# A one-core flamingo layer (cross attention and 64 experts): batch 13 routed within the last attention tiles, and loads and first steps reordered

## The reference

```python
x = x + tanh(g_xattn) * xattn(layernorm(x), ctx)      # ctx: 16 x 375 x 128
x = x + tanh(g_ffn) * ffn(layernorm(x))
# xattn: q = rope((x Wq) w_kc_q), scores with rope(ctx) over R = 64 dims, softmax, 16 heads, w_kc_kv, Wo
# ffn: router logits (64 experts), top 8, softmax of the 8; silu(gate) * up, down, weighted sum;
#      and a shared expert times sigmoid of a gate
```

## Time and profile before

| what | us |
|---|---|
| three runs | 1521.08, 1515.08, 1515.82 |
| median | 1515.82 |
| the profiled execution, its time | 1517.49 |
| its span, first to last instruction | 1515.7 |
| TensorE busy in it | 1414.5 (93%) |
| mean granted TensorE clock | 0.977 |

### The profile page before, as it was taken

One profiled execution on the slowest core, in us unless ns is written; L12 is line 12 of the kernel. 1 busy time (PEld: TensorE's weight loads), 2 busy tenths in 40 slices (PEclk: granted clock), 3 DMA queues, 4 the chain that ended last, 5 costly groups with the idle time before them and its releaser, 6 DMA issues.

```text
span 1515.7 us, 25085 instructions
## 1 busy us (share of the span) xinstructions
PE 1414.5 (93%) x7682; PEld 1159.0 (76%) x7682; DVE 1147.5 (76%) x2602; ACT 672.3 (44%) x1558; POOL 781.9 (52%) x857
## 2 busy tenths in 40 slices
PE   6999899999999999999999999986499999989987
PEld 5767788877788787778887768865389998989743
DVE  5777785298988279988539988545488999989588
ACT  3332684011377011177301137331377787767521
POOL 4555674055676458877347886326144343334322
PEclk9999999999999999999999999997699999999999
DMA  8899896456698767740267762396899999999598
GB/s 250 295 317 321 263 286 190 136 177 190 209 293 254 245 200 246 251 125 8 95 226 230 240 225 88 96 351 211 247 341 312 349 355 359 372 342 344 204 426 365
DMA packets 164648, 380.10 MB, mean 251 GB/s; under 512 B 20233, under 2 KB 55715, under 8 KB 162723
## 3 DMA queue, kind: packets, MB, share of 16 engines
q1 hardware_dynamic: 136470, 286.33, 56.9%
q0 software_dynamic: 20608, 62.28, 12.0%
q10 hardware_dynamic: 7436, 29.88, 5.9%
HBM read 238.82 MB, written 139.59 MB: 250 GB/s over the span
## 4 chain that ended last, share of the span: by engine, by line
PE 72%; DMA 10%; DVE 9%; issue 4%; POOL 3%; ACT 2%; SPq 1%; POOLq 0%; ACTq 0%; DVEq 0%
PE bank L828 18%; PE bank L830 17%; PE bank L829 17%; PE bank L932 9%; DMA p_in<-parts 4%; PE bank L961 4%; PE bank L1130 2%; DMA w_ex<-in_w_ex 2%; DMA parts<-y_sb,to_row 2%; POOL slot_rows L1991 1%; PE bank L920 1%; PE bank L1046 1%; PE bank L910 1%; DVE prob_t0l L1320 1%; ACT prob L1734 1%
## 5 line engine op out<-in xcount | busy, mean ns | idle before, releaser
L1969 POOL TENSOR_TENSOR q_rope<-q_rope,q_sin 128x448 f32<-128x448 f32 x192 | 215.4, 1151 | 127.4 <-DVE q_sin L1285 127.1
L2049 POOL DMA_INDIRECT parts<-y_sb,to_row x140 | 137.6, 983 | 222.2 <-ACT y_sb L1875 192.9
L1975 POOL TENSOR_TENSOR prob<-prob,row_inv 128x375 f32<-128x375 f32 x219 | 176.7, 813 | 89.5 <-DVE row_inv L1307 87.1
L1285 DVE TENSOR_TENSOR q_sin<-bank,sin_q 128x448 f32<-128x448 f32 (+1 forms) x256 | 158.0, 617 | 4.0
L1991 POOL DMA_INDIRECT slot_rows<-rows,pos_i x112 | 110.0, 982 | 97.4 <-DVE count L1395 70.0
L932 PE MATMUL bank<-q_rope,m_w 128*128 128x448 f32 x384 | 155.7, 541 | 2.8 <-issue 1.8
L1299 DVE TENSOR_REDUCE row_max<-bank 128x1 f32<-128x375 f32 x224 | 118.5, 534 | 37.7 <-PE bank L830 37.3
L1734 ACT ACTIVATE prob<-bank,row_max 128x375 f32<-128x375 f32 x224 | 128.3, 573 | 9.1 <-DVE row_max L1299 9.1
L1875 ACT ACTIVATE y_sb<-bank,own 96x512 f32<-96x512 f32 (+4 forms) x140 | 91.2, 687 | 68.8 <-PE bank L830 61.1
L961 PE MATMUL bank<-ident,prob 128*125 128x128 f32 x672 | 113.5, 278 | 8.5 <-DVE prob_t0l L1320 4.3
L1281 DVE TENSOR_TENSOR q_rope<-bank,cos_q 128x448 f32<-128x448 f32 x192 | 117.6, 613 | 0.0
(11 more groups left out here) (369 smaller groups left out, 4387.4 us busy)
## 6 DMA issues: line engine op xcount, KB each, us to landing
w_ex<-in_w_ex SPq DMA_DIRECT2D x64, 768.0 KB, 8.7
slot_rows<-blank SPq DMA_DIRECT2D x64, 612.0 KB, 7.5
p_in<-parts SPq DMA_DIRECT2D x13, 2048.0 KB, 16.8
m_w<-m_dram SPq DMA_DIRECT2D x48, 192.0 KB, 3.4
x_g<-slot_rows ACTq DMA_DIRECT2D x16, 476.0 KB
wq_s0h<-wq_dram SPq DMA_DIRECT2D x24, 256.0 KB, 3.6
wq_s0l<-wq_dram SPq DMA_DIRECT2D x24, 256.0 KB, 3.9
wq_s1h<-wq_dram SPq DMA_DIRECT2D x24, 256.0 KB
```

The source lines that it names most:

```text
L1285: dve.tensor_tensor(q_sin[to:to + size, other, :].rearrange("p (b s) -> p b s", b=GB), src[at:at + size], table, ALU.mult).then_inc(s_rope, 1)
L1969: pool.tensor_tensor(o[:, c, :], o[:, c, :], q_sin[:, c, :], ALU.add).then_inc(s_radd, 1)
L1975: pool.tensor_tensor(prob[i][:], prob[i][:], row_inv[:, i:i + 1].to_broadcast([P, L]), ALU.mult)\
L2049: pool.indirect_dma_start(parts, bass.IndirectOffsetOnAxis(ap=to_row[x % NROW][0:size, t:t + 1], axis=0), y_sb[x % NY][t][0:size, :], None)\
```

## The change

The start: -0.5 is a memset on POOL instead of a DMA; SP loads x of batches 0 and 2, then the identity; ACT's queue loads 1 and 3. DVE takes all statistics and norms of the four batches first, without waiting for the identity; the norms of batches 2 and 3 go into `rows` tiles. Context 1 is loaded in head 12 (the 13th) of group 0. Keeps and statistics of batches 12 to 14 are spread over tiles; batch 13 is routed, ranked, placed and scattered within the tiles and no longer beside the last pass; the last pass writes bank 2. Batch 15's statistics on POOL stand behind the first store of batch 14. The experts begin with turn(0), inner(0), turn(1), down(0).

```diff
-            sp.dma_start(ident[:], a["c_ident"]).then_inc(s_first, 16)
-            sp.dma_start(minus_half[:], a["c_minus_half"]).then_inc(s_first, 16)
...
-            for b in range(GB):
-                load_x(b)
+            load_x(0)
+            load_x(2)
+            sp.dma_start(ident[:], a["c_ident"]).then_inc(s_first, 16)
...
+            for b in (1, 3):
+                act.dma_start(x_sb[b][:], a["x"][b * S:(b + 1) * S, :]).then_inc(s_x[b], 16)
             split_wq(0)
...
+            pool.memset(minus_half[:], -0.5).then_inc(s_half, 1)
...
+        def xn1_of(b):
+            return rows[b - 2][:, 0:C] if 2 <= b < GB else xn1[b % 2][:]
...
-            dve.wait_ge(s_first, 32)
+            for b in range(GB):
+                stats_x(b)
+            for b in range(GB):
+                norm_x(b)
+            for b in range(GB):
+                turn_x(b)
+            dve.wait_ge(s_first, 16)
             for part in (*kv_t[0], *kv_t[1]):
...
+                    if g == 0 and h == X_AT:
+                        load_context(1)
...
-                        if t == 0 and g == 0:
-                            load_context(1)
...
     if p == NG:
-        return [B - 3, B - 2]
+        return [B - 2]
...
-          NG: ({"turn": 4, "router": 5, "rank": 9}, {"turn": 7, "router": 10, "rank": 15})}.get(
+          NG: ({"turn": 4, "router": 5, "rank": 9},)}.get(
...
-LATE = {HALF + 1: ("norm", FIRST_LATE), HALF + 2: ("turn", FIRST_LATE), HALF + 3: ("norm", FIRST_LATE + 1),
-        HALF + 4: ("router", FIRST_LATE), HALF + 5: ("choose", FIRST_LATE), HALF + 6: ("norm", FIRST_LATE + 2),
-        HALF + 7: ("rank", FIRST_LATE), HALF + 8: ("place", FIRST_LATE), HALF + 9: ("scatter low", FIRST_LATE),
-        HALF + 11: ("scatter high", FIRST_LATE)}
+STATS_AT = 1
+LATE = {HALF: [("keep", FIRST_LATE), ("stats", FIRST_LATE)],
+        HALF + 1: [("keep", FIRST_LATE + 1), ("norm", FIRST_LATE)],
+        HALF + 2: [("keep", FIRST_LATE + 2), ("turn", FIRST_LATE), ("stats", FIRST_LATE + 1)],
+        HALF + 3: [("stats", FIRST_LATE + 2)], HALF + 4: [("router", FIRST_LATE), ("norm", FIRST_LATE + 1)],
+        HALF + 5: [("choose", FIRST_LATE)], HALF + 6: [("norm", FIRST_LATE + 2)],
+        HALF + 7: [("rank", FIRST_LATE)], HALF + 8: [("place", FIRST_LATE)],
+        HALF + 9: [("scatter low", FIRST_LATE), ("turn", FIRST_LATE + 1)], HALF + 10: [("router", FIRST_LATE + 1)],
+        HALF + 11: [("scatter high", FIRST_LATE), ("choose", FIRST_LATE + 1)],
+        HALF + 12: [("rank", FIRST_LATE + 1), ("place", FIRST_LATE + 1), ("scatter low", FIRST_LATE + 1),
+                    ("scatter high", FIRST_LATE + 1)]}
...
 def out_bank(b):
+    if b == LAST:
+        return 2
...
                     pe.wait_ge(s_exp, RT * B)
-                    pe.wait_ge(s_route, NR * (B - GB) + R_RANKED)
...
+                    elif b == B - GB + 1:
+                        pe.wait_ge(s_route, NR * (b - 1) + R_RANKED)
...
                 for b in held(g if g < NG - 1 else NG):
-                    if b == LAST - 1:
-                        finish("stats", LAST)
-                    finish("scatter low", b)
-                    finish("scatter high", b)
+                    for k in range(TOP):
+                        if b == LAST - 1 and k == STATS_AT:
+                            finish("stats", LAST)
+                        finish(f"scatter {k}", b)
...
             turn(0)
-            for x in range(E + 1):
+            inner(0)
+            turn(1)
+            down(0)
+            for x in range(1, E + 1):
                 if x + 1 < E:
                     turn(x + 1)
                 if x < E:
                     inner(x)
-                if x >= 1:
+                if x >= 2:
                     down(x - 1)
```

More of the change, by code:

```diff
@@ L213, in route_banks @@
     if b in held(NG):
-        return 0, 1 + b % 2, 3
+        return 0, 1, 3
     if b in left_over(b // GB):
@@ L751, in sync @@
                         load_early()
-                    if g == NG - 1 and LATE.get(t):
-                        finish(*LATE.get(t))
+                    for step, b in LATE.get(t, ()) if g == NG - 1 else ():
+                        finish(step, b)
                     if t < GB * RT:
                         b, i = g * GB + t // RT, t % RT
-                        if t == 0 and g == 0:
-                            load_context(1)
                         if i == 9 and b + 2 < B:
@@ L840, in turn_x @@
                 for j in range(CJ):
-                    m = pe.transpose(bank[x_bank(b)][:, j * S:(j + 1) * S], xn1[b % 2][:, j * P:(j + 1) * P],
+                    m = pe.transpose(bank[x_bank(b)][:, j * S:(j + 1) * S], xn1_of(b)[:, j * P:(j + 1) * P],
                                      ident[0:S, 0:S])
@@ L1061, in finish @@
                     pe.matmul(bank[7][:, E:2 * E], total[:], at_place[:], start=True, stop=True).then_inc(s_total, 1)
-            pe.wait_ge(s_first, 32)
+            pe.wait_ge(s_first, 16)
             for b in range(GB):
@@ L1339, in project_out @@
                 for b in PASSES[p]:
[L1340 removed]
+                    if p < NG - 1:
                         keep_x2(b)
[L1342 to L1343 removed]
             def keep_x2(b):
@@ L1433, in vector @@
             dve.memset(count[:], 0.0).then_inc(s_pad, 1)
-            for b in range(GB):
-                stats_x(b)
-            norm_x(0)
-            norm_x(1)
-            for b in range(GB):
-                turn_x(b)
-                if b + 2 < GB:
-                    norm_x(b + 2)
             for g in range(NG):
@@ L1477, in vector @@
                             put_in_place(b)
-                        project_out(NG - 1)
-                    if g == NG - 1 and LATE.get(t):
-                        finish(*LATE.get(t))
+                    for step, b in LATE.get(t, ()) if g == NG - 1 else ():
+                        finish(step, b)
                     if attend_at(t - 1):
@@ L1573, in vector @@
             split_expert(0)
-            turn(0)
-            find_own(0)
             dve.tensor_scalar(l_room, bank[7][0:1, E:2 * E], float(-TR), 0.0, ALU.add, ALU.max).then_inc(s_rounds, 1)
@@ L1581, in vector @@
             dve.tensor_tensor(starts[:], l_at, l_first, ALU.add).then_inc(s_rounds, 1)
-            for x in range(E + 1):
+            turn(0)
+            split_expert(1)
+            inner(0)
+            find_own(0)
+            turn(1)
+            find_own(1)
+            for x in range(1, E + 1):
                 if x + 1 < E:
@@ L1879, in scalar @@
             turn(0)
-            for x in range(E + 1):
+            split_expert(1)
+            inner(0)
+            turn(1)
+            load_slots(act, NXE)
+            down(0)
+            for x in range(1, E + 1):
                 if x + 1 < E:
@@ L1976, in normalise @@
                         .then_inc(s_scaled["pool"], 1)
-            def project_out(p):
-                if p == NG - 1:
-                    for b in PASSES[p]:
-                        spread(ln_stats[b % GB], s_bn2, s_rs2, b)
             def finish(step, b):
```

13 lines of the change are left out of this document (4 added, 9 removed).

## The result

The changed kernel ran at 1509.13 us in the median of 13 runs (1503.54 to 1516.91), the kernel before beside it at 1519.18 of 13; ratio **0.9941**, 95% interval 0.9926 to 0.9956, by the ratio a gain of 9.0 us (the medians differ by 10.05). It was forecast at 1500.8, with a range of 1497.0 to 1507.7: the sign was right, the size too large. The profiled execution took 1509.13 us, its span 1507.3 against 1515.7. Two more series of the changed kernel, made later, gave 0.9953 and 0.9957.

What follows compares the result with a forecast made beforehand. TensorE, busy 93% of the span, was taken as the bound, winnable only where it waits or runs at low clock. 1.5 + 5.5 + 6.2 + 1.8 = 15.0 us gave 1502.5 profiled, 1500.8 as median; range 1497.0 to 1507.7.

Steps and rivals of the forecast that it cites:

- Part 1: The start: earlier x loads 0.5 us and a TensorE wait removed 1.0 us, together 1.5 us; bounds 0.9 and 2.3.
- the other bound: The start: if x0 lands alone first, everything moves forward by 0.92 us, instead of the 0.5 taken.
- TensorE's 1.00 us wait goes: The start: norms of batches 2 and 3 get tiles of their own, so TensorE's wait between 10.90 and 11.90 disappears.
- Part 2: Group 0's attention: context 1 loaded in the 13th head, first tile's turn to context's 11.30 us, not 16.80; gain 5.5 us.
- Part 3: Last attention part and scatters: last store 6.2 us earlier, from terms of 3.4 and 2.8; bounds 3.4 and 7.1.
- the first term: The scatters: POOL's 3.66 us wait for batch 13's place goes, less the usual 0.30, saving 3.4 us.
- The second: Last attention part: spread keeps bring batch 12's norm and placing forward; 2.8 us taken, bounds 0 and 3.7.
- the tail starts no earlier: Rival: DVE's queue from first keep to placing 12 is the bound; scatters gain only 3.4 us, 1503.6; chance 0.13.
- The step on batch 15: The scatters: batch 15 placed at 1052.8, POOL ending batch 14's stores at 1053.2, 0.4 us apart.
- Part 4: First experts: expert 0's products run in TensorE's wait for expert 1's tokens; gain 1.8 us, bounds 0 and 3.4.
- the first experts win nothing: Rival: expert 3's weights land where they did or later; 1502.6; chance 0.11.
- the sentence on the weights: First experts: expert 4's load freed some 5 us earlier, but expert 5's tokens go out 3 us earlier, sharing the engines.

Runs made afterwards that it cites:

- only_start: The kernel before with the new start alone: ratio 0.9997 (0.9984 to 1.0009) to the kernel before.
- after_third: The changed kernel run again without any edit, beside the better version on the same chip: ratio 0.9957 (0.9936 to 0.9977) to the kernel before.
- only_exp: The kernel before with the new order of the first experts alone: ratio 1.0008 (0.9992 to 1.0025) to the kernel before.

## Why the prediction was wrong

**What bounds the kernel** held: what was saved ahead of TensorE's full stretches moved them forward whole, and the parts added up, as far as the intervals tell.

**Part 1**, 1.5 us: about right at 1.2 in the mean of the traces, the term mis-sized by 0.3, and in part by luck. The first norm came 1.06 us earlier where 0.5 was taken, above even the 0.92 of the other bound. The step "TensorE's 1.00 us wait goes" was more than half wrong, as 0.58 us of it stayed. The two errors nearly cancel. Of the 1.7 us at the first product (15.40 to 13.67 in the means) some 0.5 is lost again by the first rope addition. Whether the time has even the 1.2, `only_start` can't tell.

**Part 2**, 5.5 us: the mechanism as put, 11.41 us against 11.30 forecast. The size was off by 0.9: the term took 16.80 us for the old stage, where four traces have 16.10 in the mean, and the new stage has 11.51. How late a load lands differs from execution to execution; one trace gives one draw.

**Part 3**, 6.2 us: the first term, 3.4 for POOL's gap, measured 3.7. The second, 2.8 for placing 12 earlier, measured about nothing, and this is the step that failed. The rival "the tail starts no earlier" held, with its cause (VectorE's work in another order) shown in part: relieving VectorE's queue moved the store by 1.06 us, spreading the same work by 0.1. The turn of 12 was 2.0 us earlier, as walked; but the walk stopped at the turn and took what came out there for won. The two traces show where it goes. VectorE's score behind the block, before:

```profile
1012.96 0.55 DVE L1299 TENSOR_REDUCE row_max<-bank 128x1 f32<-128x375 f32 x1 [2.50 <-PE bank L830]
```

The block behind the turn begins only 1.38 us earlier (6.32 us after the first keep against 7.70), as the keep of batch 14 now stands between tiles and TensorE needs it first (0.79 us). VectorE's score comes 1.06 us earlier (10.76 against 11.82), as the block and the scores behind it run a little longer at the low level (seven of its products against six, 0.43 us apart, from 1001.5 to 1004.5). From there VectorE works without a wait, and the statistics of batch 14 (0.68 + 0.18 us) are now behind the score instead of ahead of it: the choice of 12 begins 0.10 us earlier, 15.31 against 15.41. That low level alone is worth 1.6 us, as `after_third` shows; the prediction had put 1.7 for the clock of this stretch among what could be won. The step on batch 15 was right: it was placed at 1049.14, 0.5 us ahead of its first store at 1049.64, where 0.4 had been forecast.

**Part 4**, 1.8 us: 1.5 us longer in the means of the stage (a difference within the spread of the traces) and 1.2 longer by the time of `only_exp`, so nothing or a small loss; the rival "the first experts win nothing" held. The reordering did win what it was to win at first: TensorE is 2.2 us ahead at expert 2's products (28.25 us after the last store against 30.43), and only 0.5 at expert 3's (36.21 against 36.73), behind the wait. The step that failed is the sentence on the weights: it saw that the load of expert 5's tokens goes out earlier and shares the engines, and still left 1.8 us. The load is 1.1 us earlier in the means (22.0 to 20.9 us after the last store), and expert 3's weights are there at 33.5 instead of 31.7. With these tokens asked for later the weights are there 1.2 us earlier than in the old order (30.5 in the mean of three traces). That the earlier tokens make the whole of those 1.8 us isn't shown; that tokens hold these weights back is. A part may be POOL's stores of expert 0's results: 0.38 MB of them move ahead of the landing in the changed kernel, none before, and the prediction doesn't name them.

**The base.** Of the 8.3 us between 1500.8 and 1509.13, 3.4 are the median of before: 1515.82 in the three runs shown, 1519.18 in thirteen and 1517.8 to 1520.0 in the later series. The other 4.9 are the steps above (they come to some 7 in the means of the stages, against a spread of some 2 us). Both rivals together, with that base, come to 1519.18 - 10.4 = 1508.8; I had priced each alone. The gain of 9.0 us lies inside the bounds of the sum, 8.1 to 18.8. The time fell out of the range because the range took the median of three runs as exact; and the gain is near the lower bound because the second term of part 3 and all of part 4 came to nothing.

## What to carry to other kernels

Follow an operation that is moved forward past its first consumer, to the step that sets the end of the stage; a gain at an intermediate step is one only if nothing that stands between is full. Where the DMA engines are full, each load asked for earlier was paid here by something already on its way, in whatever queue, a load or the last stores; ask which load is needed next and let the others wait. And stages of one trace that wait for loads are draws: two or three traces of the same code, even of kernels that change something else, show their spread.

## What the runs showed of the hardware that I had not expected

A load of 768 KB under way for 7.7 us was held back 2.9 us by two of 612 KB issued later from another engine's queue, which moved 0.95 MB before it landed. Weights loaded beside POOL's indirect stores left the stores' starts 1.25 us apart but delayed the landing of the last by 4.0 us (8.3 us after its start instead of 4.4). After the same two waits of 1.00 and 0.79 us TensorE ran a block of nine products at the high level in one trace of the changed kernel, and six to eight of the nine at the low level in the twelve other traces with the keeps spread; it moved the first store by 1.6 us, and what decides it these traces don't show. And the same 400 us of experts took 401.8 to 407.8 us in eighteen traces of nearly the same code, with waits for weights at different experts, a spread as wide as the largest part of this change; what makes it was not taken apart.
